# The attention gates of a row computed in the first FFN stage, and decay sums from rows shifted by half a tile

## The reference

```python
q = _swish((x @ Wq).reshape(b, t, H, K))
k = _swish((x @ Wk).reshape(b, t, H, K))
v = (x @ Wv).reshape(b, t, H, V)
f = jax.nn.log_sigmoid((x @ Wf).reshape(b, t, H, M)) / GATE_LOGIT_NORMALIZER
s = 1.0 - jnp.exp(f)
...
hk = hk * ge[:, :, None, :] + k_t[..., :, None] * s_t[..., None, :]
logits = jnp.einsum('bhk,bhkm->bhm', q_t * scale, hk)
p = jax.nn.softmax(logits, axis=-1)
hv = hv * ge[..., :, None] + s_t[..., :, None] * v_t[..., None, :]
o_t = jnp.einsum('bhm,bhmv->bhv', p, hv)
...
x = x + 0.5 * _L0_ffn_ref(_layernorm(x, axis=-1), ...)
x = x + _L0_attn_ref(_layernorm(x, axis=-1), ...)
x = x + 0.5 * _L0_ffn_ref(_layernorm(x, axis=-1), ...)
```

## Time and profile before

| | |
|---|---|
| median of 3 runs | 3081.52 us (3077.74 to 3081.72) |
| the profiled execution | 3076.98 us, span 3075.2 us, clock 0.995 |
| busy share of the span | PE 97%, DVE 85%, ACT 46%, POOL 41% |
| first FFN | from the start to some 1240 us |
| attention | some 1260 to 2165 us |
| second FFN | from some 2175 us to the end |

### The profile page before, as it was taken

The page is one execution under the profiler, slowest core; times in us unless marked ns, Lnnn a source line. Parts: engine busy times, 40 slices in busy tenths (PEclk is TensorE's granted clock), DMA queues, the critical chain, the costliest instruction groups (busy, mean ns, idle before and its releaser), DMA issues.

```text
span 3075.2 us, 97305 instructions
## 1 busy us (share of the span) xinstructions
PE 2976.7 (97%) x34688; PEld 2609.5 (85%) x34688; DVE 2602.5 (85%) x4369; ACT 1419.7 (46%) x4051; POOL 1259.9 (41%) x2168
## 2 busy tenths in 40 slices
PE   5999999999999999799999999999899999999999
PEld 4888888888888888688888888888788888888888
DVE  8888888888888887488888888888899999999998
ACT  3333333333333333788888888887222222222222
POOL 4333333333333333255555555555433333333332
PEclk9999999999999999999999999999999999999999
DMA  4444444444444443444444444444332222222222
GB/s 111 119 124 125 125 124 124 124 123 123 123 123 123 123 123 115 126 129 132 133 132 135 133 132 131 131 133 127 92 77 75 75 75 75 76 77 77 76 77 58
DMA packets 485055, 340.86 MB, mean 111 GB/s; under 512 B 301940, under 2 KB 451828, under 8 KB 484984
## 3 DMA queue, kind: packets, MB, share of 16 engines
q1 hardware_dynamic: 484984, 339.91, 39.0%
HBM read 155.19 MB, written 117.44 MB: 89 GB/s over the span
## 4 chain that ended last, share of the span: by engine, by line
PE 93%; issue 2%; DVE 2%; ACT 1%; POOL 0%; DMA 0%; DVEq 0%; SPq 0%; POOLq 0%; ACTq 0%
PE banks L472 37%; PE banks L700 22%; PE banks L1196 7%; PE banks L1167 5%; PE banks L712 4%; PE banks L1192 4%; PE banks L680 3%; PE banks L678 3%; PE banks L1230 3%; PE banks L1157 2%; PE banks L1251 1%; PE banks L1283 1%; DVE masked L1052 1%; PE banks L1245 1%; DVE att_x_out L1134 0%
## 5 line engine op out<-in xcount | busy, mean ns | idle before, releaser
L700 PE MATMUL banks<-ffn_xT_hl,w_hl 128*128 128x128 f16 x12288 | 730.1, 219 | 0.0
L472 PE MATMUL banks<-w_hl,midT_hl 128*128 128x256 f16 x6144 | 712.6, 273 | 6.1 <-DVE low_hl L628 5.5
L700 PEld LDWEIGHTS banks<-ffn_xT_hl,w_hl 128*128 128x128 f16 x12288 | 704.5, 98 | 3.9 <-issue 0.6
L556 ACT ACTIVATE midT_hl<-banks 128x1024 f16<-128x1024 f32 x256 | 261.9, 1023 | 903.8 <-PE banks L712 903.8
L472 PEld LDWEIGHTS banks<-w_hl,midT_hl 128*128 128x128 f16 x6144 | 594.8, 98 | 75.9 <-DVE midT_hl L622 7.3
L249 POOL TENSOR_TENSOR ffn_var_eps<-ffn_moments,eps_col 128x1 f32<-128x1 f32 x256 | 94.1, 367 | 1270.7 <-DVE ffn_moments L245 1270.7
L601 DVE TENSOR_TENSOR_SCAN runmax<-restart,banks 128x1024 f32<-128x1024 f32 x256 | 585.4, 2287 | 8.8 <-PE banks L680 1.0
L622 DVE SCALAR_TENSOR_TENSOR midT_hl<-banks,midT_hl 128x1024 f16<-128x1024 f32 x256 | 312.6, 1221 | 193.8 <-ACT midT_hl L556 193.8
L606 DVE TENSOR_TENSOR step<-runmax 128x1024 bf16<-128x1024 f32 x256 | 314.8, 1230 | 8.9
L472 PE MATMUL banks<-wqkfv_hl,att_xT_hl 128*128 128x512 f16 (+1 forms) x1536 | 292.2, 326 | 1.5 <-DMA att_xT_hl<-att_xn_hl 1.5
L265 ACT ACTIVATE ffn_xn_hl<-ffn_xc,ffn_rstd 128x256 f16<-128x256 f32 x256 | 129.3, 505 | 307.7 <-POOL ffn_xc L256 292.1
(11 more groups left out here) (137 smaller groups left out, 5765.2 us busy)
## 6 DMA issues: line engine op xcount, KB each, us to landing
projected<-qkvf_out SPq DMA_DIRECT2D x128, 512.0 KB, 2.9
qkv<-projected SPq DMA_DIRECT2D x128, 384.0 KB, 3.3
x_in<-in_L_attn_x SPq DMA_DIRECT2D x128, 128.0 KB, 2.7
x_res<-in_L_attn_x SPq DMA_DIRECT2D x128, 128.0 KB, 2.1
x<-x_out SPq DMA_DIRECT2D x128, 128.0 KB, 2.0
gate<-projected SPq DMA_DIRECT2D x128, 128.0 KB, 3.1
att_x_res<-x SPq DMA_DIRECT2D x128, 128.0 KB, 2.1
x<-att_x_out SPq DMA_DIRECT2D x128, 128.0 KB, 1.7
```

The source lines that it names most:

```text
L472: last = nc.tensor.matmul(dst, left(lp, k), right(rp, k), start=(k == 0 and lp == rp), stop=(k == blocks - 1 and lp == 1))
L556: nc.scalar.activation(midT_hl[:, t.slot, 0], mid_ps[t.slot], ACT.Relu).then_inc(mid_high_made, 1)
L700: nc.tensor.matmul(mid_ps[t.slot][:, cols], w1_hl[:, wp, k, cols], xT_hl[:, t.ring, xp, k], start=(c % PER_BANK == 0 and k == 0 and wp == xp),
```

## The change

Abs, exp, ln, `logsig`, the f16 split and the exp for `keep` of a row are done in the first FFN, on the gate that the projection has just left in SBUF (`qkvf_out[:, slot, 3]`). The result, 2 KB a token (the two f16 halves in one float row, and exp), goes to DRAM as `gates_d`; `projected` keeps q, k and v. Each row of the first FFN now switches the activation tables twice. Attention loads a row's gates, and for rows with a state behind them it loads the f16 halves a second time, from 64 tokens earlier (`mixed`): the decay sum then is one sum over all tokens of one tile, with one matrix `ones16`.

```diff
+                def store_gates(t):
+                    after(sp, S["gate_low"], t)
+                    sp.dma_start(gates_by_tile[t.row], gates_out[:, t.slot]).then_inc(gates_stored[t.slot], 16)
...
                 def swish(t):
-                    if is_late(t, ROWS_BESIDE_ATTENTION - 1):
-                        nc.scalar.preload_act_table_set("silu_and_others")
+                    nc.scalar.preload_act_table_set("silu_and_others")
                     after(act, qk_projected, t)
...
-                    if is_late(t, ROWS_BESIDE_ATTENTION):
-                        nc.scalar.preload_act_table_set("natural_log_exp_and_others")
+                    nc.scalar.preload_act_table_set("natural_log_exp_and_others")
+
+                def gate_softplus(t):
+                    after(act, vf_scaled, t)
+                    nc.scalar.activation(absgate[:, t.slot], qkvf_out[:, t.slot, 3], ACT.Abs
+                                         ).then_inc(S["gate_abs"], 1)
+                    after(act, S["gate_abs"], t)
+                    nc.scalar.activation(absgate[:, t.slot], absgate[:, t.slot], ACT.Exp, scale=-1.0
+                                         ).then_inc(S["gate_exp"], 1)
+                    after(act, S["gate_exp"], t)
+                    after(act, S["gate_logsig"], t, lag=2)
+                    nc.scalar.activation(lnone[:, t.slot], absgate[:, t.slot], ACT.Ln, bias=1.0
+                                         ).then_inc(S["gate_ln"], 1)
+
+                def gate_high(t):
+                    after(act, S["gate_logsig"], t)
+                    after_dma(act, gates_stored, t, lag=2)
+                    nc.scalar.activation(gates_out[:, t.slot, 1], logsig[:, t.slot], ACT.Exp, scale=GATE)
+                    nc.scalar.activation(halves_of(gates_out[:, t.slot])[:, 0], logsig[:, t.slot], ACT.Copy
+                                         ).then_inc(S["gate_high"], 1)
...
-                              (swish, -5), (first_only(round_attention, act), -1)]
+                              (swish, -5), (gate_softplus, -5), (gate_high, -6),
+                              (first_only(round_attention, act), -1)]
...
-                    stages = [(finish, -2), (lambda t: norm.stats(dve, t), 5),
+                    stages = [(finish, -2), (gate_logsig, -6), (lambda t: norm.stats(dve, t), 5),
...
+                    stages += [(lambda t: norm2.centre(pool, t), -2), (gate_low, -7),
...
+                def load_mixed(t):
+
+                    if t.chunk:
+                        after_chunk(sp, S["decay_col_done"], t, LATER, lag=4)
+                        sp.dma_start(mixed[:, t.ring], mixed_rows[t.row - 1, :, 0:1]
+                                     ).then_inc(mixed_loaded[t.ring], 16)
...
-                return Phase([(load_residual, -4), (load_qkv, 2), (load_gate, 6), (store, -5), (turn_o, -3)],
+                return Phase([(load_residual, -4), (load_qkv, 2), (load_gates, 4), (load_mixed, 4), (store, -5),
+                              (turn_o, -3)],
...
                     if t.chunk:
-                        terms = [(late16, past), (early16, now)]
-                        for n, (ones, gates) in enumerate(terms):
-                            for part in range(2):
-                                last = nc.tensor.matmul(decay_ps, ones[:, :], gates[:, part],
-                                                        start=(n == 0 and part == 0), stop=(n == 1 and part == 1))
+                        after_ring_dma(pe, mixed_loaded, t)
+                        between = halves_of(mixed[:, t.ring])
+                        for part in range(2):
+                            last = nc.tensor.matmul(decay_ps, ones16[:, :], between[:, part],
+                                                    start=(part == 0), stop=(part == 1))
```

More of the change, by code:

```diff
@@ L172, in build @@
         ramp16 = sb("ramp16", [P, P], f16)
-        late16 = sb("late16", [P, P], f16)
-        early16 = sb("early16", [P, P], f16)
+        ones16 = sb("ones16", [P, P], f16)
         causal = sb("causal", [P, P])
@@ L795, in attention_phase @@
             qkv = fb("qkv", [P, 4, 3, D])
-            gate = fb("gate", [P, 4, D])
-            absgate = fb("absgate", [P, 2, D])
-            lnone = fb("lnone", [P, 2, D])
-            logsig = fb("logsig", [P, 2, D])
-            gate_hl = fb("gate_hl", [P, 4, 2, D], f16)
-            keep = fb("keep", [P, 4, D])
+            gates = fb("gates", [P, 4, 2, D])
+            mixed = fb("mixed", [P, 4, 1, D])
             expG = fb("expG", [P, 4, D])
@@ L1258, in log_gate_sums @@
                         for a in range(PAIRS):
-                            for n, (ones, gates) in enumerate(terms):
-                                for part in range(2):
-                                    last = nc.tensor.matmul(col_ps[:, a:a + 1],
-                                                            gates[:, part, a * P:(a + 1) * P], ones[:, 0:1],
-                                                            start=(n == 0 and part == 0),
-                                                            stop=(n == 1 and part == 1))
+                            for part in range(2):
+                                last = nc.tensor.matmul(col_ps[:, a:a + 1],
+                                                        between[:, part, a * P:(a + 1) * P], ones16[:, 0:1],
+                                                        start=(part == 0), stop=(part == 1))
                         last.then_inc(S["decay_col_done"], 1)
@@ L1297, in build, with halves_of @@
         qkvf_stored, qkvf_ps = pair("qkvf_stored"), bank(7)
+        gates_stored = pair("gates_stored")
+        def halves_of(gates):
+            return gates[:, 0].bitcast(f16).rearrange("p (n d) -> p n d", n=2)
         S = {n: sem(n) for n in (
-            "gate_abs", "gate_exp", "gate_ln", "gate_logsig", "gate_high", "gate_low", "keep_made",
+            "gate_abs", "gate_exp", "gate_ln", "gate_logsig", "gate_high", "gate_low",
             "G_done", "expG_made", "expnG_made", "decay_rows_made", "decay_own_made",
```

96 lines of the change are left out of this document (40 added, 56 removed).

## The result

The changed kernel takes **3051.81 us** (median of 4 runs, 3051.63 to 3053.97) against 3081.62 of the kernel before (3077.74 to 3082.57): ratio 0.9907, 95% interval 0.989 to 0.9924. It is 30 us faster. The forecast was 3082, no change; its range, 3043 to 3090, holds the time. What happened is the rival that had a chance of 0.24: `St` comes first in both steps.

The account below looks back on a forecast made before the run. TensorE was taken to bound the first FFN; in attention its transposes wait for `St`, which races `decay_own`. First FFN 0, handover -2 and attention +4 gave +2 us: forecast 3082, range 3043 to 3090.

Parts of the forecast that it names:

- the rival that had a chance of 0.24: Attention: `St` comes before `decay_own` in steps 0 and 1; -1.07 us a sequence, 3043 profiled or 3047 median; chance 0.24.
- The sum of five intervals: Attention, steps 0 and 1: predicted starts put GpSimd's `decay_own` 0.02 us ahead of VectorE's `St`.
- the race: Attention, between pairs of transposes (a step): `St` and `decay_own` exclude each other in SBUF; whichever comes first holds the other.
- the one likeliest case: Attention: `decay_own` first in steps 0 and 1; 27.83 instead of 27.70 a sequence, +4 us in all; chance 0.45.
- one of each: Attention: `St` first in one of steps 0 and 1, `decay_own` in the other; -0.47 a sequence, 3061 to 3066; chance 0.23.
- Attention, VectorE: Attention: L1027 goes; step 1 gains 0.04 us, step 2 nothing; in step 0 `state_sum` can start at 1727.20, not 1727.71.
- Attention, PE: Attention: matmuls worth 0.3 us go in three steps of four, mostly into waiting; busy time falls about 29 us.
- The first FFN stage: 0: First FFN stage: added ScalarE, VectorE and GpSimd work fits idle time, PE stays busy; 0 us.
- ScalarE becomes the bound: First FFN stage: ScalarE limits rows beyond 1.1 us more each than counted; 3090 to 3120, or 3280 with drain; chance 0.05.
- The handover: -2: Between first FFN and attention: ScalarE's 0.49 us wait for `logsig` disappears in four rows; -2 us.
- The late loads: Attention: SyncE's additional load per step and later gate stores make loads late; 3090 to 3100 us; chance 0.03.

Follow-up runs that it names:

- e12: Changed kernel with a tiny VectorE memset ahead of the reciprocal that precedes `St`; 3055.48 us, ratio 0.9921.
- e1: Changed kernel with a tiny VectorE memset right ahead of `St`, behind the reciprocal; 3086.75 us, ratio 1.0028.
- e6: Changed kernel with an idle VectorE operation of `logsig`'s size put back at its old place; 3072.67 us, ratio 0.9982.
- e5: Kernel before with one tiny GpSimd operation ahead of `decay_own` in each step; 3063.84 us, ratio 0.9951.
- e2: Changed kernel with decay sums made as before from both rows' gates, without the second, shifted load; 3057.45 us, ratio 0.9933.
- e7: Changed kernel with two more activation table loads in each row of the first FFN; 3152.29 us, ratio 1.0238.
- e3: Changed kernel with `make_St` ahead of `o_low` and `invert_totals` in VectorE's list; 3022.62 us, ratio 0.9821.
- e10: Changed kernel with the reciprocal ahead of `St` over 32 columns instead of 4; 3094.77 us, ratio 1.0051.
- e9: Changed kernel with the reciprocal ahead of `St` over 16 columns instead of 4; 3057.96 us, ratio 0.9935.

## Why the prediction was wrong

**The step that failed** is this one: "So GpSimd is ahead of `St` by 0.02 in both steps; by the earlier trace rows 0.01 was enough." Its first half was good. The sum of five intervals gave `St` 0.02 behind `decay_own` in both steps, and the trace shows 0.00 and 0.01. The second half was not. The earlier trace rows is another VectorE operation against another GpSimd operation, and it was read as a law of the pair of engines. For `St` behind its reciprocal over 4 columns 0.03 was not enough (e12), and 0.08 was. The rows at hand for this very pair bounded the turning point only between -0.16 and 0.10, and 0.02 lies inside. They gave no ground for 0.45 on one outcome against 0.24 on the other. That the race went to `St` is shown; why a recorded start of 0.00 to 0.01 behind is early enough stays open, so the rival's outcome was not foreseen by a better argument but was one of two that the rows left open. The chances were nearer to it than the number: they put 0.50 on faster, while 3082 was the time of the one likeliest case.

**The price of either outcome** was right. With `St` first: steps 6.83 and 6.35 and a sum of 26.63 forecast, 6.82, 6.32 and 26.59 measured. With `decay_own` first: 7.43, 6.95 and 27.83 forecast, 7.42, 6.93 and 27.83 in e1, which has the memset besides. The rival's "one of each", 27.23 or 27.24, is e6: 27.21.

**Attention, VectorE.** That step 1 and step 2 wait for PE and gain next to nothing from `logsig`'s removal while step 0 gains is shown by e6: step 1 6.82 with and without it. The 1.06 that step 0 gains split in three: 0.51 is the race (7.38 to 6.87, e5), 0.30 the earlier `St` (6.87 to 6.57, from e5 to e2, where PE's own work becomes the limit), and 0.25 PE's smaller work (e2 to the changed kernel).

**Attention, PE.** "Work removed, little of it time": PE's busy time fell by 30 us (29 forecast), and by e2 some 6 us of that were time. The prediction has the transposes of step 0 wait for `St`. With `St` first they do not: PE has no idle time in that step, 6.32 is its own work, and that is where the 6 us come from.

**The first FFN stage: 0** was right. PE is busy throughout and a row takes 9.57. The gap of 1.11 that is left ahead of L571 is the 1.1 of the prediction. The rival "ScalarE becomes the bound" is real, but it starts later than the 1.1 us a row that the prediction gave it: by e7 at 1.9.

**The handover: -2** was wrong in sign: it cost 4.0 (3 to 7 over the runs that have the gate work in the first FFN, e7 left out). I counted what ScalarE does in those rows (the same loads, one wait less) and not what stands behind it on its queue. The gate's five operations moved from behind `kT_StT` to ahead of it, and PE waits for `kT_StT` 9.7 us there instead of 4.3, of which shorter waits elsewhere give back a part. This is read from the rows; no run moved those operations back.

**The last rows** lose 2.0 where 0 was forecast. In the last two steps `St` loses the race in the changed kernel and takes 0.9; that is 0.30 and 0.55 of it, and the rest was not looked for.

The rival's total was 3043 on the profiled execution, and it took 3051.9. The 9 are made up of 1.5 in the first rows of the launch, 6.0 at the handover (+4.0 for -2), 2.0 at the end and -0.5 in the steps. The late loads (chance 0.03) did not show.

## What to carry to other kernels

Where VectorE and GpSimd meet in every period, compute both outcomes of the race and give them near equal chances unless the margin is over 0.1 us in rows of that very pair; better still, take the operation that TensorE waits for out of the race, since here an order of three stages (46 us) was worth more than moving the work (30). When work moves to another stage, follow it at the seam as well: whose wait stands behind it on its new queue. And test a change again once the wait it relieves has been relieved in a cheaper way: of the moved gate work nothing was left, while the second load gained more than before.

## What the runs showed of the hardware

- Of `St` and `decay_own`, whichever is kept out ends a fixed time after the one that kept it out, whenever it was itself recorded to start: a held `St` ends 0.28 after `decay_own`, in all runs, and a held `decay_own` 0.58 to 0.60 after the VectorE operation (it takes 0.81 in step 1 of the kernel before, 0.99 in the changed kernel, and 0.92 in e3, where `o_low` holds it). The Trainium skill ("SBUF — State Buffer", SBUF: two separate sides) says of a VectorE operation with two inputs in SBUF and a GpSimd operation that reads SBUF that whoever starts first keeps the other out for its whole instruction, and all runs agree with that. The prediction's "two operations that both work in SBUF" is too wide: the reciprocal, which has one input, runs beside `decay_own` in e10 (from 1767.24 for 0.35, `decay_own` from 1767.32 for 0.73), and neither is held.
- "Starts first" cannot be read from the recorded starts within 0.1 us. Behind the reciprocal over 4 columns `St` won when recorded up to 0.03 behind and lost from 0.08 on; behind the one over 16 columns it won at up to 0.09 and lost at 0.17, in the first and last steps of attention in e9. Right behind a memset it lost at 0.01 (27 of 29 times in step 0 of e1, with a recorded start ahead of the memset's own), and L1094 of the kernel before lost at 0.01 too. What in the instruction ahead decides it stays open.
- VectorE's reciprocal on 128 partitions takes 0.17 us over 4 columns, 0.25 over 16 and 0.35 over 32, about 6 ns a column, so an edit of 12 columns was no 12 ns.
